# A graph kernel on one core: 62 of 3126 row gathers are taken over by SyncE as single-row DMAs

## The reference

```
h = relu(layernorm(x))
x = x + L0(h)          # two graph convolutions and a dense layer
h = relu(layernorm(x))
x = x + L1(h)          # attention over 4 heads; only the edges 0..12499 and their rows are used

L0: h = h @ W_pre + b_pre
    h = relu(conv(h, W1, b1));  h = relu(conv(h, W2, b2));  y = h @ W_post + b_post
conv(x, W, b): norm = dinv[src] * dinv[dst]          # self loops added, dinv = deg ** -0.5
               out[dst] += (x @ W)[src] * norm;  out + b
```

## Time and profile before

| | |
|---|---|
| median of 3 runs | 4140.42 us (4136.22 to 4140.93) |
| span of the profiled execution | 4132.4 us |
| median less span | 8.0 us |
| first convolution's gathers | from 111.2 us to about 2067 us |
| second convolution's gathers | from about 2081 us to 4037 us |
| POOL busy | 3025.7 us, 73% |
| TensorE busy | 3066.6 us, 74% |
| DMA engines | 124 GB/s mean |

### The profile page before, as it was taken

The page is one execution under the profiler, slowest core; times in us unless marked ns, Lnnn a source line. Parts: engine busy times, 40 slices in busy tenths (PEclk is TensorE's granted clock), DMA queues, the critical chain, the costliest instruction groups (busy, mean ns, idle before and its releaser), DMA issues.

```text
span 4132.4 us, 36624 instructions
## 1 busy us (share of the span) xinstructions
PE 3066.6 (74%) x12107; PEld 1945.3 (47%) x12107; DVE 1279.2 (31%) x2593; ACT 392.7 (10%) x1088; POOL 3025.7 (73%) x3173
## 2 busy tenths in 40 slices
PE   6677777777776777777777777777778877777778
PEld 6344444443443443344444554444445555555556
DVE  8222222222222222222222233332224444434456
ACT  7000000000000000000001111111111111111112
POOL 3677777777777777777767777777777777777773
PEclk9878888888889888888879889999998899999988
DMA  8444444444444444444434444443334444444455
GB/s 268 135 118 118 118 119 119 118 119 120 119 118 119 118 121 118 119 119 118 121 100 119 119 118 121 118 118 112 113 113 120 117 118 118 115 121 129 118 153 176
DMA packets 248738, 513.99 MB, mean 124 GB/s; under 512 B 62491, under 2 KB 141832, under 8 KB 248296
## 3 DMA queue, kind: packets, MB, share of 16 engines
q0 software_dynamic: 150048, 410.73, 35.6%
q1 hardware_dynamic: 98504, 100.82, 8.2%
HBM read 471.70 MB, written 39.64 MB: 124 GB/s over the span
## 4 chain that ended last, share of the span: by engine, by line
POOL 66%; issue 22%; DMA 5%; PE 4%; DVE 1%; ACT 1%; SPq 0%; POOLq 0%; DVEq 0%
POOL sb_big L956 66%; DMA sb_big<-T,sb_srci 4%; PE bank L1241 2%; PE bank L570 1%; PE bank L1728 0%; ACT sb_big L791 0%; PE bank L1703 0%; PE bank L1713 0%; DVE sb_big L857 0%; DMA T<-sb_big 0%; PE bank L550 0%; DVE sb_big L859 0%; DMA sb_work<-dstT 0%; POOL sb_X L1900 0%; DVE sb_looks L668 0%
## 5 line engine op out<-in xcount | busy, mean ns | idle before, releaser
L956 POOL DMA_INDIRECT sb_big<-T,sb_srci x3126 | 2960.4, 947 | 975.9 <-issue 943.3
L1241 PE MATMUL bank<-sb_big 128*128 (+2 forms) x7056 | 2511.2, 463 | 987.8 <-DMA sb_big<-T,sb_srci 938.1
L1241 PEld LDWEIGHTS bank<-sb_big 128*128 128x128 f32 x7056 | 1303.3, 216 | 1954.6 <-issue 1816.3
L1001 DVE SCALAR_TENSOR_TENSOR sb_big<-sb_dstf,bank 128x2304 f32<-128x2304 f32 x196 | 499.0, 2546 | 29.9 <-issue 29.8
L1031 DVE SCALAR_TENSOR_TENSOR sb_work<-sb_bW,sb_work,bank 128x256 f32<-128x256 f32 x98 | 47.2, 481 | 1292.3 <-PE bank L1168 1292.3
L1016 DVE TENSOR_TENSOR sb_work<-bank,sb_work 128x257 f32<-128x257 f32 (+1 forms) x196 | 83.2, 425 | 461.3 <-PE bank L1241 461.3
L1040 DVE SCALAR_TENSOR_TENSOR sb_work<-bank,sb_dinv,sb_b 128x256 f32<-128x256 f32 x98 | 47.4, 484 | 529.3 <-PE bank L1168 529.3
L1070 ACT COPY sb_work<-bank 128x256 f32<-128x256 f32 x196 | 73.0, 373 | 1263.9 <-PE bank L1129 1263.9
L1050 DVE TENSOR_TENSOR sb_X<-sb_X,bank 128x256 f32<-128x256 f32 x98 | 41.2, 421 | 390.2 <-PE bank L1181 390.2
L1079 ACT ACTIVATE sb_work<-sb_work,sb_dinv 128x256 f32<-128x256 f32 x98 | 49.9, 509 | 878.4 <-DVE sb_work L1032 878.4
L1128 PE MATMUL bank<-sb_ident,sb_work 128*128 128x128 f32 x392 | 118.7, 303 | 16.9 <-DVE sb_work L1040 11.9
(11 more groups left out here) (200 smaller groups left out, 1719.7 us busy)
## 6 DMA issues: line engine op xcount, KB each, us to landing
sb_big<-T,sb_srci POOLq DMA_INDIRECT x3126, 2.8
sb_work<-T SPq DMA_DIRECT2D x49, 257.0 KB
T<-sb_work SPq DMA_DIRECT2D x49, 256.0 KB, 2.4
sb_work<-T SPq DMA_DIRECT2D x49, 256.0 KB
sb_X<-x SPq DMA_DIRECT2D x13, 896.0 KB, 11.1
out<-sb_X SPq DMA_DIRECT2D x9, 1024.0 KB
T<-sb_big SPq DMA_DIRECT2D x8, 899.5 KB, 6.0
sb_looks<-LO SPq DMA_DIRECT2D x23, 256.0 KB
```

The source lines that it names most:

```text
L956: pool.indirect_dma_start(out, None, table, bass.IndirectOffsetOnAxis(idx, 0)).then_inc(s.g[u % NSEM], 16)
L1001: v.scalar_tensor_tensor(t.S[:, b * K:(b + 1) * K, :], t.dstf[:, bass.ds(tj, K)].unsqueeze(2).to_broadcast([P, K, P]), float(-P * j), psum ...
L1241: mm = pe.matmul(ps.A[b][:, 0:w], t.S[:, b * K + k, :], rhs, start=(k == 0), stop=(k == K - 1))
```

## The change

SyncE takes over the fetching of 31 chunks in each convolution. The chunks are number 88, 136, 184 and so on, every 48th, up to 1528. For each, SyncE issues 128 DMAs of one row each (1028 bytes of T1 or 1024 of T2) to one partition of a waiting slot ("lane"), of which there are four. The row's address is in a register: the chunks' src values come in a new input `srcS`, VectorE multiplies them by the row size in bytes, and SyncE loads up to 32 of them at a time into registers (`reg_load`). 43 rows are issued in each step of `sp_node_tiles`, from step 0 to step 92. ScalarE copies the full lane into the ring slot of the chunk at the end of `act_sum` of step 3, 6, 9 and so on up to 93, after waiting for the 128 rows and for the slot. TensorE waits for this copy (`chunk_wait`) where it waited for the gather. GpSimd skips these chunks. The ring has 40 slots for 44, so that lanes and ring take the room of the ring before. `sp_low` now stands ahead of the rows of step 0, in which SyncE also waits until the addresses are scaled. The row semaphores are ones that the fast path did not use.

```
-RING = 44
+RING = 40
+LANES = 4
+SLOTS_ALL = RING + LANES
...
+ROW_RATES = ((P, 0, (43, 1), 24), (P, 0, (43, 1), 24))
+LAST_COPY = 94
+REGS_A_LOAD = 32
...
+def lane_tables():
+
+    lists, steps, copies, e0 = [], [], [], 0
+    for c in range(2):
+        sp, act, per, delta = ROW_RATES[c]
+        rows, at, n = [], [], 0
+        while True:
+            last = max(ceil((n + 1) * sp / per[0]), ceil((n + 1) * act / per[1]) + 1 if act else 0)
+            e = P // 8 * (last + 1) + delta
+            if last > LAST_COPY:
+                break
+            rows.append(e)
+            at.append(last)
+            n += 1
+        lists.append(rows)
+        copies.append(at)
+        for eng, (lo, hi) in enumerate(((0, sp), (sp, P))):
+            step = [[] for _ in range(NT)]
+            for r in range(len(rows) * (hi - lo)):
+                step[r // per[eng]].append((r // (hi - lo), lo + r % (hi - lo)))
+            steps.append(step)
+    return lists, steps, copies
...
+def chunk_wait(eng, s, u):
+    if u in LANE_OF:
+        eng.wait_ge(s.copied, LANE_OF[u] + 1)
+    else:
+        eng.wait_ge(s.g[u % NSEM], landed(u))
...
+def lane_rows(eng, t, s, a, which, c, j):
+
+    table, w = ((a.T1, TW), (a.T2, D))[c]
+    flat = table.rearrange("n d -> (n d)").bitcast(U8)
+    todo = LANE_STEPS[2 * c + which][j]
+    while todo:
+        n, p = todo[0]
+        m = next((k for k, (q, _) in enumerate(todo) if q != n), len(todo))
+        m = min(m, REGS_A_LOAD)
+        u = n + len(LANE_CHUNKS[0]) * c
+        if u >= LANES:
+            eng.wait_ge(s.copied, u - LANES + 1)
+        regs = [eng.alloc_register(f"lane{which}_{c}_{j}_{n}_{p + k}") for k in range(m)]
+        q = LIST0 + BY_ROW.index(LANE_CHUNKS[c][n])
+        eng.reg_load(regs, t.offsets[c][q:q + 1, p:p + m])
+        for k in range(m):
+            at = eng.snap(regs[k], donate=True, min_val=0, max_val=4 * w * (N - 1))
+            eng.dma_start(t.lane[p + k:p + k + 1, u % LANES, 0:w].bitcast(U8),
+                          flat[bass.ds(at, 4 * w)].unsqueeze(0)).then_inc(s.rows[u % LANES], 16)
+        todo = todo[m:]
...
+def act_lane(act, t, s, i):
+
+    c, j = divmod(i, NT)
+    w = (TW, D)[c]
+    for e, at in zip(LANE_CHUNKS[c], LANE_COPIES[c]):
+        if at == j:
+            u = LANE_OF[c * ET + e]
+            act.wait_ge(s.rows[u % LANES], 16 * P * (u // LANES + 1))
+            act.wait_ge(s.agg, released(c * ET + e - RING))
+            act.copy(t.ring[:, (c * ET + e + OFF) % RING, 0:w], t.lane[:, u % LANES, 0:w]).then_inc(s.copied, 1)
...
+def dve_offsets(v, ch, t, s):
+    v.wait_ge(s.listed, 16)
+    lists = slice(LIST0, LIST0 + len(BY_ROW))
+    ch.step(v.tensor_scalar(t.offsets[0][lists], t.offsets[1][lists], 4 * TW, None, ALU.mult))
+    v.tensor_scalar(t.offsets[1][lists], t.offsets[1][lists], 4 * D, None, ALU.mult).then_inc(s.scaled, 1)
...
@@ pool_conv
     for u in range(c * ET, (c + 1) * ET):
+        if u in LANE_OF:
+            continue
...
@@ act_sum
     act.copy(t.YT[:, i % 2, :], ps.T[:, 0:D]).then_inc(s.TC, 1)
+    if fast:
+        act_lane(act, t, s, i)
...
@@ pe_sums
-            gather_wait(pe, s, c * ET + seen)
+            chunk_wait(pe, s, c * ET + seen)
...
@@ dve_fast
     dve_onehot(v, ch, t, s, ps, 1)
+    dve_offsets(v, ch, t, s)
...
@@ sp_node_tiles
         if b and j + 1 < NT:
             load(j + 1)
+        if fast and c == 0:
+            if j == 0:
+                sp_low(sp, t, s, a)
+                sp.wait_ge(s.scaled, 1)
+            lane_rows(sp, t, s, a, 0, c, j)
         rows = slice(j * P, (j + 1) * P)
...
-            if fast and j == 0:
-                sp_low(sp, t, s, a)
...
                 sp_looks(sp, t, s, a, j + 2)
+                lane_rows(sp, t, s, a, 0, c, j)
...
@@ program, sync
+                sp.dma_start(t.offsets[1][LIST0:LIST0 + len(BY_ROW)], a.srcS).then_inc(s.listed, 16)
                 wait_table1(sp, s, 0)
```

More of the change, by code:

```diff
@@ L13 @@
 I32 = mybir.dt.int32
+U8 = mybir.dt.uint8
 BF16 = mybir.dt.bfloat16
@@ L190, in views @@
     t.X = sb("X", [P, NT, D])
-    big = sb("big", [P, RING * TW + 2 * K * P])
+    big = sb("big", [P, SLOTS_ALL * TW + 2 * K * P])
     t.srci = sb("srci", [P, ET + 1], I32)
@@ L203, in views @@
     t.bp = sb("bp", [P, D])
-    t.onesr = sb("onesr", [1, P])
+    ones = sb("ones", [P, P])
+    t.onesr = ones[0:1, :]
     t.onesc = sb("onesc", [P, 1])
@@ L217, in views @@
     work = sb("work", [P, WORK])
-    t.ring, _ = take(big, 0, [RING, TW])
-    t.ring3, _ = take(big, 0, [RING * TW // XW, XW])
-    t.S, _ = take(big, RING * TW, [2 * K, P])
+    t.lane, o = take(big, 0, [LANES, TW])
+    t.ring, _ = take(big, o, [RING, TW])
+    t.slots, _ = take(big, 0, [SLOTS_ALL, TW])
+    t.ring3, _ = take(big, 0, [SLOTS_ALL * TW // XW, XW])
+    t.S, _ = take(big, SLOTS_ALL * TW, [2 * K, P])
     o = 0
@@ L232, in views @@
     t.OH = [v, u] * (NOH // 2 - 1) + [v, w]
-    assert last <= STAGE_SLOT[2] * TW and (STAGE_SLOT[2] + GROUP) * TW <= RING * TW - SPILL
+    assert last <= STAGE_SLOT[2] * TW and (STAGE_SLOT[2] + GROUP) * TW <= SLOTS_ALL * TW - SPILL
     t.bpx, _ = take(looks, 0, [2 * P])
-    assert o <= RING * TW - SPILL, o
+    assert o <= SLOTS_ALL * TW - SPILL, o
     t.loi = t.srci[:, :].rearrange("p (t i) -> p t i", t=2)
@@ L244, in views @@
             t.junk.append(v[:, k * P:(k + 1) * P].bitcast(BF16))
-    o = RING * TW - SPILL
+    o = SLOTS_ALL * TW - SPILL
     t.lob, o = take(big, o, [2, NPAIR], BF16)
@@ L263, in views @@
     t.rowi, _ = take(looks, 1000, [100], I32)
-    assert o <= RING * TW + 2 * K * P, o
+    assert o <= SLOTS_ALL * TW + 2 * K * P, o
     o = 0
@@ L272, in views @@
     t.zero7, o = take(big, o, [P], BF16)
-    assert o <= RING * TW, o
+    assert o <= SLOTS_ALL * TW, o
     o = 0
@@ L306, in views @@
     t.stage = [staged[:, k, :].rearrange("p (j d) -> p j d", d=TW) for k in range(2)]
-    t.stage += [t.ring[:, k:k + GROUP, :] for k in STAGE_SLOT[2:]]
+    t.stage += [t.slots[:, k:k + GROUP, :] for k in STAGE_SLOT[2:]]
     o = 0
@@ L322, in views @@
     t.lowb, o = take(looks, o, [2, P], BF16)
+    scaled, o = take(looks, o, [P], I32)
+    t.offsets = [scaled, ones[:, :].bitcast(I32)]
     t.alf, o = take(t.Wc[:, :, :].rearrange("p c d -> p (c d)"), 0, [NT, 4])
@@ L339, in views @@
     t.prodd, o = take(big, o, [2, 512])
-    assert o <= RING * TW, o
-    t.maskd, o = take(big, RING * TW, [NT * PD])
+    assert o <= SLOTS_ALL * TW, o
+    t.maskd, o = take(big, SLOTS_ALL * TW, [NT * PD])
     t.same32, o = take(big, o, [NT, WIN], BF16)
-    assert o <= RING * TW + K * P
-    t.M, o = take(big, RING * TW + K * P, [4, BATCH * P])
-    assert o <= RING * TW + 2 * K * P
+    assert o <= SLOTS_ALL * TW + K * P
+    t.M, o = take(big, SLOTS_ALL * TW + K * P, [4, BATCH * P])
+    assert o <= SLOTS_ALL * TW + 2 * K * P
     t.MT, o = take(work, 0, [4, BATCH * P])
@@ L466, in semaphores @@
     s.fput = [s.fput0, s.fput1]
+    s.rows = [s.fg0, s.fg1, s.fcur0, s.fcur1]
+    s.copied, s.scaled, s.listed = s.fput0, s.fput1, s.fin
     return s
@@ new lines, with first_need @@
+LANE_CHUNKS, LANE_STEPS, LANE_COPIES = lane_tables()
+LANE_OF = {c * ET + e: sum(map(len, LANE_CHUNKS[:c])) + n for c in range(2) for n, e in enumerate(LANE_CHUNKS[c])}
+BY_ROW = sorted({e for rows in LANE_CHUNKS for e in rows})
+LIST0 = 64
+assert len(BY_ROW) <= P - LIST0
+def first_need(c, e):
+    return next((j, k) for j in range(NT) for k in range(K) if min(UB[j] + k, ET - 1) >= e)
+for c, (rows, at) in enumerate(zip(LANE_CHUNKS, LANE_COPIES)):
+    for e, j in zip(rows, at):
+        assert released(c * ET + e - RING) <= NTH * (c * NT + j + 1), (c, e, j)
+        assert first_need(c, e) > (j + 1, PLACE1[0] + 1), (c, e, j, first_need(c, e))
@@ new lines, in landed @@
+def landed(u):
+    return 16 * sum(1 for v in range(u % NSEM, u + 1, NSEM) if v not in LANE_OF)
+def chunk_wait(eng, s, u):
[22 more added lines that the diff above has]
+        todo = todo[m:]
@@ L1342, in dve_fast2, with act_fast @@
     dve_end(v, ch, t, s, ps)
-def act_fast(act, t, s, ps):
+def act_fast(act, t, s, ps, a):
     for i in range(NT):
@@ L1348, in act_fast, with act_fast2 @@
         act_hidden(act, t, s, ps, i, True)
-    act_fast2(act, t, s, ps)
-def act_fast2(act, t, s, ps):
+    act_fast2(act, t, s, ps, a)
+def act_fast2(act, t, s, ps, a):
     last = NT + NCLOSE
@@ L1620, in sp_node_tiles @@
                 sp_looks(sp, t, s, a, j + 2)
+                lane_rows(sp, t, s, a, 0, c, j)
 NLOOK = len(PHASES) * NB
-EARLY = (FIRST_SLOT[1] + LB[NT - 2]) % RING * TW // (P // 2)
-assert EARLY < NT and (FIRST_SLOT[1] + LB[NT - 1]) % RING * TW >= NT * P // 2
+EARLY = (LANES + (FIRST_SLOT[1] + LB[NT - 2]) % RING) * TW // (P // 2)
+assert EARLY < NT and (LANES + (FIRST_SLOT[1] + LB[NT - 1]) % RING) * TW >= NT * P // 2
 SPREAD = ((0, 20), (20, 20), (40, 20), (60, 20), (80, 18))
@@ L2210, in _ @@
             with act.If(regular(act, s, t)):
-                act_fast(act, t, s, ps)
```

(3 more changed lines are left out.)

## The result

The changed kernel takes 4538.5 us (median of 4 runs, 4537.4 to 4539.9), the kernel before 4140.2 beside it: a ratio of 1.097 (1.095 to 1.098). The forecast was 4066 with a range up to 4190. It came out on the side of the first rival, "SyncE becomes the bound".

A forecast was written before the change was run, and what follows sets the result against it. The prediction took GpSimd's gathers, one every 1.25 us, to bound the kernel, with SyncE's 18.3 us step hidden under 19.5. 77.6 - 2 - 1 = 74.6 us off 4140.4 gave 4066 us, range 4058 to 4190.

The forecast's parts named there:

- SyncE becomes the bound: Rival: SyncE's step above 20.2 us; dear register words about 5050 us, chance 0.10, or crowded rows about 4660, chance 0.10.
- Register loads: Two per SyncE step, about 1 us each, 2.0 us in all; ends 1.0 and 8.8 us.
- Rows: SyncE's 43 one-row DMAs a step at 0.37 us each: 15.9 us; ends 14.2 and 21.9.
- SyncE's own DMAs: SyncE's loads and stores of tiles, with waits: 0.4 us of its 18.3 us step.
- The crowded price of the rows: Rival in SyncE's step: rows at 0.48 us, step 23.0 us, +520, about 4660 us; chance 0.10.
- 62 gathers are worth 77.6 us: Gathers leaving GpSimd: 62 x 1.251 = 77.6 us gained, all ahead of tile 96.
- Which way SyncE's lateness goes: If SyncE's step is too long, ScalarE's copy waits for rows, TensorE for ScalarE, and POOL follows SyncE.
- My "2 us" for the tail: About 2 us off the gain, as the last chunk, number 1528, is used where TensorE no longer waits.
- gathers slow down: Rival: gathers beside the rows 0.017 us slower on average, 52 us given back, about 4118 us; chance 0.10.
- Copies: 62 copies on ScalarE at 0.37 us each, 23 us on a little-used engine: costs nothing.
- Ring of 40: Ring of 40 slots for 44: POOL still has free slots ahead, so it costs nothing.
- Skipped gathers not on the path: Rival: the gathers taken from GpSimd gain nothing, 4140 us; chance 0.02.

The follow-up runs named there:

- g2: Changed kernel with each register load begun at the multiple of 4 words at or below its first row: 4080.5 us, 0.984 of the kernel before.
- h1: Aligned loads as in g2, plus the last copy in step 90, so 60 chunks by rows for 62: 4062.4 us, 0.982 of the kernel before.
- h2: Changed kernel with a chunk's rows dealt 44, 44, 40 over three steps and last copy in step 90: 4058.0 us, 0.981 of the kernel before.
- h3: Changed kernel without register loads, rows from fixed addresses (wrong rows in 62 chunks), on a chip without the gaps: 4067.4 us, 0.983 of the kernel before.
- h4: Changed kernel with no chunk by rows, GpSimd gathering all 3126, ring still 40, on a chip without the gaps: 4136.4 us, 1.000 of the kernel before.
- e2: Changed kernel without register loads, rows from fixed addresses (wrong rows in 62 chunks), first series: 4774.6 us, 1.0015 of the kernel before.
- f2: The kernel of e2 run again in a second series on another chip: 4735.3 us, 1.0007 of the kernel before.
- e1: The kernel of g2, loads begun at a multiple of 4 words, in the first series: 5611.7 us, 1.178 of the kernel before.
- e4: Changed kernel with no chunk by rows, GpSimd gathering all 3126, ring still 40, first series: 4761.5 us, 0.998 of the kernel before.
- e3: Changed kernel with a chunk's rows dealt 44, 44, 40 over three steps, first series: 5679.7 us, 1.191 of the kernel before.

## Why the prediction was wrong

*Register loads:* this is the term that failed, "the nearest in size is the one of 16 words ... words cost little and a load about 1 us: 2.0 us per step". Measured 7.5 us a step, near the upper end of 8.8 that I had written and set aside. The 7-word row already had both prices in it. Of VectorE's 28 loads eight took 1.03 to 1.08 us, exactly those that begin at word 0, 28, 56 or 84, multiples of 4; the other twenty took 1.62 to 1.64. TensorE's 28 loads of the same words divide in the same way, 1.06 to 1.09 and 1.70 to 1.72. The 16-word row was the wrong one to go by: all of its loads begin at a multiple of 4, only three of its six loads of 16 words took 1.11 us and the others 1.39 to 1.72, and the seventh, of 2 words, took 1.08, so that most of the figure is not the words' price. The changed kernel's loads begin at all four places, three of four off the boundary. I gave the dearer price a chance of 0.10 and a time of 5050.

*Rows:* 13.8 us for my 15.9 (0.322 us each for 0.37). *SyncE's own DMAs:* 1 us for my 0.4, as 0.2 us a step of short gaps was not in it. So the errors in SyncE's sum had opposite signs; 18.3 against a measured 22.4. With the loads at 3.5 us (g2) the sum is 18.3 by luck, the rows being 2.1 us cheaper and the rest 2.1 us dearer than I had them, and the kernel is faster. The crowded price of the rows (0.48) did not come.

*62 gathers are worth 77.6 us:* right, as soon as SyncE keeps up (h1, h2, h3 and g2, each within 3 us of what its own count gives).

*Which way SyncE's lateness goes:* half right. I named the copy's rows; the other engines waited longer for the pair load and the T2 store behind the rows (1146.5 and 794.9 us of waiting, against 620.8). My "2 us" for the tail missed a queue: the rows of the last steps stand behind look-up loads that wait, 14.7 us. I had counted what stands behind the rows, and not what the rows stand behind.

*Do the rows slow GpSimd's gathers?* No: 947 ns before, 948 with 7936 rows beside them, 946 in h2. The value taken, 0, was right, and so the rival "gathers slow down" falls.

*Copies:* 406 ns each for my 372, hidden in g2 but for two waits of 28.5 us in all, 25.1 of it in tile 94. *Ring of 40:* nothing, as said (h4: 1.000, 0.999 to 1.001). *DMA engines:* SyncE's queue is at 9.2% in g2 for 8.2%, with two packets more for each row and not 16: as by bytes (0.7%) and not the 10.6% of rows cut over all 16. *Skipped gathers not on the path:* falls, by h1 to h3.

The Trainium skill's rule in "Runtime: NRT & Kernel Launch", "Instruction fetch mechanics", gives about 200 ns per register even in bulk. The page says it of loads from HBM; the words here lie in SBUF. It spoke against the change, and I let one row outweigh it. The traces bear it out for loads that begin off a multiple of 4 words, (6.91 - 0.52) / 31 = 0.206 us a word, and not for the others.

## What to carry to other kernels

Before work is moved to an idle engine, price each instruction that it will issue by a row of the same kind on that engine; where two rows disagree, look for what tells them apart before one is chosen, and see whether the step stays under the pace at the upper end too. Begin bulk register loads at a multiple of 16 bytes and make their length a multiple of 4 words. And keep work that others wait for from standing behind loads that wait themselves, in the last steps above all: h1 did it by leaving that work out, and no run tried another order.

## What the runs showed of the hardware that I had not expected

A register load on SyncE costs by where it begins. Means by number of words, off the boundary from the trace of the changed kernel, on it from the changed and the aligned kernel together (390 loads each; the numbers of words come from the kernel's own order):
```
words                              1     2     3     5     7     11    32
begins off a multiple of 4, us    0.52  0.71  0.91  1.32  1.72  2.59  6.91
words                              4     7     8     11    16    24    32
begins on a multiple of 4, us     0.57  1.19  0.78  1.44  1.28  1.76  2.19
```
About 0.2 us a word off the boundary, and nearly the same one, two or three words off it; on it about 0.23 us for each four words, and 0.2 for each word left over: 7 words cost more than 8. The largest group is that of 32 words, 6.65 to 7.53 us off the boundary (108 loads), 2.03 to 2.80 on it (190). VectorE and TensorE show the same division in their loads of 7 words (above).

SyncE also shows a gap of 0.34 us every 128 instructions in the changed kernel, 126 of them, 42.6 us in all; these are the 0.34 us of "issue" in its chain. The queue for instructions has 200 packets where the kernel before has 74, 126 more, as many as the gaps. That SyncE waits there for its own instructions fits this, but no run tested it.

The gaps of the first two chips stay open. There the kernel before took 15% longer (4769 and 4733 us for 4140), and the kernels with rows and register loads lost another 17 to 19%, while the one with rows alone (e2, f2) kept level. It is not that its SyncE stops less: with half as many instructions it has 1946 gaps, 1288 us in all, beside e1's 2104 and 1369. But its step has room for them. In h3_static SyncE waits 6.3 us of each step of 19.6; in e2_static, from 300 to 1900 us, its step is 23.0 us with 0.5 of waiting left, and the kernel without rows needs 23.1 us a tile there by itself. SyncE's 435 instructions in that kernel (e4) have no such gap.

TensorE's mean granted clock was lower there too, 0.75 in e4_ring40 for 0.88 in h4_ring40, the same kernel. It doesn't account for the time: the sums' matrix products took 444 ns in the mean there and 461 here. What stops the two engines, and why VectorE and ScalarE don't stop, wasn't found; 45% of the chain that ended last in e4_ring40 is put down to "another core or an unknown queue", so the trace leaves open what was waited for. The aligned kernel is 1.6% faster where there are no gaps (g2) and 18% slower where there are (e1). h2 was not run on such a chip; e3, which differs from it only in the last chunks, was 19% slower there.
